# A GNN layer on one core: the two halves of the weights stored interleaved, column by column

## What is computed

```python
def reference(x, adj, item_feat, W_item, b_item, W_user, b_user):
    # x, item_feat: 10000 x 128; adj: 10000 x 10000, float32
    u = maximum(layernorm(x), 0)
    h = item_feat @ W_item.T + b_item          # 10000 x 128
    b = u @ W_user.T + b_user
    return x + relu(adj @ h + b)
```

## Time and profile before

| | |
|---|---|
| median of 3 runs | 1154.68 us (1153.7 to 1154.87) |
| profiled execution | 1155.03 us |
| its span, first to last instruction | 1153.5 us |
| busy: PE / PEld | 1132.1 us / 925.8 us |
| busy: DVE / ACT | 976.4 us / 773.4 us |
| mean granted TensorE clock | 0.997 |
| HBM traffic over the span | 360 GB/s |

### The profile page before, as it was taken

How to read it: one execution, slowest core, us unless ns; L and a number is a source line. 1 busy time by engine, 2 the same in 40 slices (tenths; PEclk the granted TensorE clock), 3 DMA queues, 4 the chain that set the end, 5 groups by cost and what they waited for, 6 DMA issues and landing times.

```text
span 1153.5 us, 14338 instructions
## 1 busy us (share of the span) xinstructions
PE 1132.1 (98%) x5078; PEld 925.8 (80%) x5078; DVE 976.4 (85%) x683; ACT 773.4 (67%) x502; POOL 20.3 (2%) x42
## 2 busy tenths in 40 slices
PE   6999999999999999999999999999999999999998
PEld 5888888878888888788888887888888878888886
DVE  5989988888888888898898888888888888888886
ACT  4766767667676666576667675766666657667663
POOL 0000000000000000000000000000000000000000
PEclk9999999999999999999999999999999999999999
DMA  9999999999999999999999998999999999999993
GB/s 355 397 400 359 352 364 372 347 362 345 376 372 360 367 365 392 365 370 368 355 367 362 385 379 338 376 362 373 357 371 380 381 331 378 376 358 353 364 387 120
DMA packets 62659, 416.38 MB, mean 361 GB/s; under 512 B 7644, under 2 KB 9124, under 8 KB 62608
## 3 DMA queue, kind: packets, MB, share of 16 engines
q1 hardware_dynamic: 59984, 406.38, 92.3%
q0 software_dynamic: 2624, 9.22, 2.3%
HBM read 410.45 MB, written 5.12 MB: 360 GB/s over the span
## 4 chain that ended last, share of the span: by engine, by line
PE 96%; DVE 1%; issue 1%; ACT 1%; DMA 1%; DVEq 0%; SPq 0%; ACTq 0%
PE acc L508 61%; PE acc L514 31%; PE spare L464 2%; PE acc L497 1%; DVE y L397 1%; PE spare L490 1%; PE spare L484 1%; ACT hi_ring L277 1%; DMA items<-in_item_t 1%; DVE lo_ring L340 0%; PE acc L525 0%; DVEq L94 0%; DVEq L427 0%; SPq L199 0%; SPq L188 0%
## 5 line engine op out<-in xcount | busy, mean ns | idle before, releaser
L340 DVE TENSOR_TENSOR lo_ring<-a_ring,hi_ring 128x2000 fp32r<-128x2000 f32 x390 | 871.3, 2241 | 152.8 <-ACT hi_ring L277 151.4
L277 ACT CAST hi_ring<-a_ring 128x2000 fp32r<-128x2000 f32 x390 | 729.0, 1869 | 360.6 <-PE acc L514 357.2
L508 PE MATMUL acc<-hi_ring,h_lo 128*128 128x500 f32 x1560 | 434.6, 399 | 5.5 <-DVE y L397 4.4
L508 PE MATMUL acc<-hi_ring,h_hi 128*128 128x500 f32 x1560 | 420.0, 391 | 0.0
L514 PE MATMUL acc<-lo_ring,h_hi 128*128 128x500 f32 x1560 | 419.1, 390 | 0.0
L508 PEld LDWEIGHTS acc<-hi_ring,h_lo 128*128 128x128 f32 x1560 | 289.5, 189 | 76.4 <-DVE y L397 12.4
L514 PEld LDWEIGHTS acc<-lo_ring,h_hi 128*128 128x128 f32 x1560 | 294.2, 189 | 62.1
L508 PEld LDWEIGHTS acc<-hi_ring,h_hi 128*128 128x128 f32 x1560 | 293.9, 188 | 61.7
L464 PE MATMUL spare<-wi,items 128*128 128x128 f32 x156 | 23.9, 294 | 10.5 <-DMA items<-in_item_t 8.7
L464 PEld LDWEIGHTS spare<-wi,items 128*128 128x128 f32 x156 | 23.0, 206 | 12.9 <-issue 6.8
L345 DVE TENSOR_TENSOR h_full<-spare,bi 128x384 f32<-128x384 f32 x26 | 14.3, 551 | 10.3 <-DMA bi<-in_b_item_rows 6.6
(11 more groups left out here) (29 smaller groups left out, 113.8 us busy)
## 6 DMA issues: line engine op xcount, KB each, us to landing
a_ring<-in_adj_tiles SPq DMA_DIRECT2D x390, 1000.0 KB, 6.9
rows<-in_x_rows POOLq DMA_DIRECT2D x20, 250.0 KB, 7.6
items<-in_item_t SPq DMA_DIRECT2D x12, 384.0 KB, 7.6
out_t<-y POOLq DMA_DIRECT2D x16, 250.0 KB, 5.3
out_t<-y SPq DMA_DIRECT2D x4, 250.0 KB, 2.2
a_rem<-in_adj_rem SPq DMA_DIRECT2D x20, 31.2 KB, 4.2
items<-in_item_t SPq DMA_DIRECT2D x2, 192.0 KB, 4.9
wi<-in_w_item_t SPq DMA_DIRECT2D x1, 64.0 KB, 1.8
```

The costliest lines, as they stand in the source:

```text
L277: nc.scalar.copy(hi_ring[:, r, :], a_ring[:, s, 0:GROUP_W]).then_inc(hi_written, 1)
L340: nc.vector.tensor_tensor(lo_ring[:, r, :], a_ring[:, s, 0:GROUP_W], hi_ring[:, r, :], ALU.subtract).then_inc(lo_written[s], 1)
L508: nc.tensor.matmul(acc[k][:, 0:BANK_W], h_part[:, c, :], hi_ring[:, r, k * BANK_W:(k + 1) * BANK_W], start=(c == 0 and h_part is h_lo), st ...
```

## The change

One tensor `h_parts` takes the place of `h_hi` and `h_lo`. Its innermost dimension has two places, the rounded value and the remainder of the same column. `h_hi` and `h_lo` become views of it, in which neighbouring columns are two float32 words, 8 bytes, apart. All instructions that write or read them stay as they are in number, order and shape: L282 writes and L352 reads h_hi, L352 writes h_lo, and the weights of L508 and L514 are read from either.

```diff
-        h_hi = sb("h_hi", [P, CHUNKS, HID], F32R)
-        h_lo = sb("h_lo", [P, CHUNKS, HID], F32R)
+        h_parts = sb("h_parts", [P, CHUNKS, HID, 2], F32R)
+        h_hi, h_lo = h_parts[:, :, :, 0], h_parts[:, :, :, 1]
```

## The result

The changed kernel takes 1159.82 us in the median of six runs (1158.88 to 1160.87), against 1154.61 us for the kernel before, measured beside it. The ratio is 1.0047, with an interval from 1.0034 to 1.0060: slower by 5.2 us, a small loss but clear of zero, and above the 0.2% named in the prediction. The profiled execution took 1160.87 us with a span of 1159.3.

What follows compares the result with a forecast made beforehand. PE's 4680 adjacency matmuls at 227.5 ns each were taken to bound the kernel. 1155.03 + 4680 x 0 + 0 = 1155.0 us, forecast as 1154.7 because timed runs' median lay 0.35 lower; range 1152.5 to 1245 us.

Steps and rivals of the forecast that it cites:

- 31% for slower: Whole kernel slower by over 0.2%: disturbed matmul reading 12%, slow load reads 12%, late DVE 7%.
- the late DVE: First group: DVE late from 0.8 us more per L352, costing up to 11.2 us, 1158 to 1166 us; 7%.
- What bounds the kernel: PE's 4680 adjacency matmuls, L508 and L514, at 227.5 ns each: 1065 us, 92% of the span.
- The weight loads' reading: L508 and L514 loads: 188 ns, 107 of it reading, some 81 fixed latency; could read 2.1 times slower before setting spacing.
- 4680 x 0: The 4680 weight loads of L508 and L514: the stride adds 0 us, up to a doubling of reading time.
- hidden with 10 ns left: Load needing two read steps a column: reads 213 ns, plus 4 is 217, below the matmul spacing of 227.5.
- my own rule: On PE, loads follow one another at their reading time plus at most 4 ns.
- loads disturb the matmul's own reading: L508 and L514: strided loads add 0 to 19.2 ns a matmul, at most 90 us, 1245 us; 12%.
- Slow reads: The 4680 loads: at 2.5 read steps a column, 267 ns reading, 43.5 ns more a matmul, +204 us, 1359 us; 12%.
- The first group: Weight writes, 26 L282 on ACT and 26 L352 on DVE: +0.2 us on each, 0 on the path.
- each column twice: Upper bound for weight writes: 0.43 us more per L352 on DVE, 0.36 per L282 on ACT; neither on the path.
- The Trainium skill's two rules: SBUF: 16-byte line hit twice gives full bandwidth, +0. VectorE: needs adjacent pairs; carried to loads, 175 to 254 ns, upper +143 us.

Runs made afterwards that it cites:

- 24 bytes: Against the kernel before: h_hi and h_lo of a trio of chunks interleaved column by column, weights of a matmul 24 bytes apart; 1186.22 us, ratio 1.0274.
- 12 bytes: Against the kernel before: a trio of chunks interleaved, h_hi and h_lo in tensors of their own, weights 12 bytes apart; 1167.86 us, ratio 1.0114.
- the by-chunk kernel: Against the kernel before: 128 columns of h_hi, then 128 of h_lo, interleaved chunk by chunk, each matmul's weights side by side; 1154.91 us, ratio 0.9999.
- the first attempt: Kernel before with first and last chunk bank by bank, remainder matmul behind each bank, DVE emptying earlier: packed 1172.19 us (1.0159), strided 1168.08 us (1.0129).

## Why the prediction was right and where it was wrong

The time lies in the stated range, but not where the forecast put it: it was one of the 31% for slower, while 66% stood on no change, within 1152.5 to 1157 us. The whole range held 1159.8 us only because it was drawn out to 1245 for a rival at 12%. The rival of the late DVE had 1158 to 1166 us, but not by its mechanism: L352 kept its time. Point by point:

*What bounds the kernel* was right: time per matmul decides, and half a nanosecond was named as what would make the forecast fail. It was 0.66 over a whole group.

*The weight loads' reading* was judged rightly in size: reading 107 ns, latency 81, and a cover that ends at about a doubling. At 24 bytes the load grew by 120 ns, and the kernel by 32 us, not by the 501 us that it would cost uncovered.

*The step that failed is the term 4680 x 0.* I let a load that fits below the matmul cost nothing. It isn't so: the spacing moved by 0.4 to 0.7 ns for the 7 ns at 8 bytes, and by 2.0 ns (229.4 - 227.4) for 65 ns at 12 bytes, where some 50 ns of cover are left. At 24 bytes it moved by 5.1 ns, but there the load reads 227 ns, not the 213 that I called hidden with 10 ns left, and by my own rule the cover is used up. Of the rivals, "loads disturb the matmul's own reading" (12%) names this, at a price of 0 to 19.2 ns that was far too wide above: it is 0.66 ns, some 3 us in all. Whether the load disturbs through the extra lines that it touches or through its length, the runs don't separate.

*A term that the sum lacks is the clock.* The rows behind the groups' ends showed it (0.83 behind two of four, and the earlier trace rows stand in one of them), and I counted only its mean, 0.997. A fall behind a group's end costs up to 1.5 us. With the falls gone from both kernels the loss is 3.3 us instead of 5.2 to 5.7, so some 2 us hang on the group's end. Matmuls added to packed weights brought extra loss too: of the increase over the kernel before, these parts were in no instruction: 2.7 - 4 x 0.32 = 1.4 us with half of the chunks strided (groups of 223.19 us), 3.0 - 4 x 0.34 = 1.6 with three matmuls more at the end (223.21), and 5.2 - 4 x 0.64 = 2.6 with three in the middle (223.51).

What decides whether the clock falls stays open. It isn't the length of the group by itself: the profiles at 12 and 24 bytes, whose groups without a fall take 225.4 and 228.9 us, have two falls each, like the kernel before, and the by-chunk kernel, with the length of before, has three in its profile (1156.12 us, its slowest execution, at an unchanged median). It isn't the wait for DVE alone: the first attempt had none and fell. Shown is that both kernels kept the full clock once PE had neither that wait nor narrow matmuls between the wide ones of a chunk. The number of falls varies between executions, and one profile doesn't give it.

*Slow reads* (12%) didn't come: 196 ns, not 267 + 81.

*The first group* was right. I took +0.2 us on each of the 52 writes and nothing on the path; it was 0.03 us on ACT and 0.001 on DVE, and the first group ends 0.26 us later. My upper bound, each column twice, is about what 24 bytes gave: 0.41 us more on DVE and 0.44 on ACT (958 and 951 ns in the mean), where 0.43 and 0.36 were worked out, so for ACT it was too low.

*The Trainium skill's two rules.* The rows at 12 and 24 bytes speak for the Trainium skill's "SBUF — State Buffer", Specifications (TRN2). By its rule, a word alone in its 16 bytes should cost. At 24 bytes all 128 words are alone: +120 ns, 0.94 ns a word. At 12 bytes, four words lie in 48 bytes, two of them sharing a line, so 64 are alone: +65 ns, 1.0 ns a word. At 8 bytes none is alone: +7 ns, small but not nothing. The rule of the Trainium skill's "Vector Engine (DVE) Microarchitecture Reference", section 5.2, that VectorE needs adjacent pairs, doesn't hold here at a distance of 8 bytes: L352 writes and reads every other word in 553 ns, as when packed. At 24 bytes it takes 958 ns. The table of that section begins, without pairs, at 1.71 ns a column and not at the 1.73 of the prediction; no term hangs on it.

## What to carry to other kernels

A weight load that fits beside the bounding matmul isn't free for that: where thousands of pairs run side by side, ask what half a nanosecond on each would cost, and widen the sum by it. Keep the float32 words of a weight load at most 8 bytes apart. Where PE waits at a regular place, read the granted clock behind each of those places and not the mean, and try to take the wait away without setting narrow matmuls between wide ones: here it was worth 1.1%, more than the layout costs, where the first attempt lost 1.3 to 1.6%.

## What was not expected of the hardware

- The clock falls to 1.2 GHz behind some of the waits at a group's end, though PE idles there for only 1.1 us, and costs up to 1.5 us each time. With narrow matmuls between the wide ones and no wait for DVE it fell for ten microseconds, 4.7 us each time. A kernel that adds 0.64 us of work to each of four groups loses that and about as much again, 1.1 us of it unexplained.
- Going from matmuls of 128 rows to a matmul of 17 rows and back is dear: 1.92 us for a bank that holds 0.68 us of wide matmuls and that one, with PE's loads idle for 0.74 us behind it.
- A word alone in its 16 bytes adds about 1 ns to a weight load at full clock, and 1.1 to 1.2 ns in ACT's writes; two in 16 bytes cost nearly nothing (7 ns for 128).
- With a quarter of the weight columns, the 500 moving columns still need 225.7 ns between starts, not 208.3. What holds them there is open.
